# Causal attention scores for two heads in one matmul, statistics of two heads in one instruction, and a new order in the causal loops

## What is computed

```python
q, k, v = split(x @ w_qkv)                        # 16 images, 6 heads of 16 channels, 256 tokens
s = einsum("bhqd,bhkd->bhqk", q, k) * 16 ** -0.5
a = softmax(where(k_index > q_index, -1e30, s))   # causal
y = einsum("bhqk,bhkd->bhqd", a, v)
x = x + y @ w_proj
```

## Time and profile before

| | |
|---|---|
| median of three runs | 844.55 us |
| profiled execution | 844.32 us, of which the span of the core is 842.3 us |
| TensorE, VectorE, ScalarE, POOL busy in the span | 92%, 70%, 68%, 31% |
| layer 0 and the start of layer 1 | to about 82 us |
| loop of layer 1 | about 82 to 262 us |
| causal loops of layers 2 and 3 | about 310 to 455 us and 528 to 675 us |
| experts | about 695 to 842 us |

### The profile page before, as it was taken

One profiled execution on the slowest core, in us unless ns is written; L12 is line 12 of the kernel. 1 busy time (PEld: TensorE's weight loads), 2 busy tenths in 40 slices (PEclk: granted clock), 3 DMA queues, 4 the chain that ended last, 5 costly groups with the idle time before them and its releaser, 6 DMA issues.

```text
span 842.3 us, 17768 instructions
## 1 busy us (share of the span) xinstructions
PE 774.3 (92%) x5481; PEld 595.2 (71%) x5481; DVE 591.4 (70%) x1527; ACT 576.3 (68%) x1431; POOL 263.5 (31%) x514
## 2 busy tenths in 40 slices
PE   2997999999998979999999985999999978999997
PEld 1965877878886957777776683677777676777775
DVE  6157777777775447878785996688878716787775
ACT  3334878877775447878786845688888726887775
POOL 2702365665654451112121000122112110333334
PEclk9998999999999689999999987899999977999999
DMA  6000001111111123323332003132323303121320
GB/s 208 1 1 1 1 11 20 18 16 17 20 21 19 20 76 85 102 78 102 85 91 59 1 1 74 54 100 80 101 80 98 89 1 78 48 47 61 79 49 19
DMA packets 63270, 44.47 MB, mean 53 GB/s; under 512 B 34416, under 2 KB 55280, under 8 KB 63088
## 3 DMA queue, kind: packets, MB, share of 16 engines
q1 hardware_dynamic: 63216, 43.78, 20.5%
HBM read 12.24 MB, written 3.21 MB: 18 GB/s over the span
## 4 chain that ended last, share of the span: by engine, by line
PE 54%; DVE 7%; issue 3%; POOL 2%; ACT 1%; POOLq 0%
PE ps L1172 8%; PE ps L1334 8%; PE ps L1323 8%; PE ps L1045 6%; PE ps L951 5%; PE ps L955 4%; PE ps L973 2%; PE ps L974 2%; PE ps L1017 2%; PE ps L987 2%; POOL onn L416 1%; PE ps L996 1%; PE ps L1308 1%; DVE amax L1747 1%; PE ps L1093 1%
## 5 line engine op out<-in xcount | busy, mean ns | idle before, releaser
L588 ACT ACTIVATE ee<-ps,nmax 128x128 f32<-128x128 f32 (+1 forms) x584 | 207.4, 444 | 9.9 <-DVE nmax L1502 5.1
L1172 PE MATMUL ps<-w,ee 128*128 128x128 f32 x960 | 140.9, 275 | 2.5
L1172 PEld LDWEIGHTS ps<-w,ee 128*128 128x128 f32 x960 | 113.6, 143 | 19.1 <-ACT ee L588 5.0
L1505 DVE TENSOR_REDUCE nmax<-ps 128x2 f32<-128x256 f32 x200 | 101.8, 551 | 30.0 <-PE ps L955 29.1
L575 ACT ACTIVATE big<-ps 128x512 f32<-128x512 f32 (+1 forms) x192 | 97.5, 552 | 31.6 <-PE ps L1172 30.9
L1847 DVE TENSOR_TENSOR hhl<-ee,hhl 128x512 fp32r<-128x512 f32 x96 | 79.8, 837 | 32.1 <-ACT hhl L815 30.5
L944 PE MATMUL ps<-kh,big 128*128 128x256 f32 x384 | 94.7, 391 | 1.7 <-POOL big L354 1.2
L492 POOL TENSOR_TENSOR xc<-big,xc 96x512 f32<-96x512 f32 x32 | 52.6, 1643 | 108.0 <-DVE big L1841 107.9
L1502 DVE TENSOR_REDUCE nmax<-ps 128x4 f32<-128x1024 f32 x48 | 58.7, 1223 | 39.1 <-PE ps L944 38.6
L1323 PE MATMUL ps<-qk,w1hl 128*128 128x512 f32 x288 | 85.0, 406 | 0.4 <-DVE ee L1850 0.4
L1334 PE MATMUL ps<-hhl,w2hl 128*96 128x512 f32 x288 | 83.4, 400 | 0.3 <-DVE hhl L1847 0.3
(11 more groups left out here) (264 smaller groups left out, 1375.4 us busy)
## 6 DMA issues: line engine op xcount, KB each, us to landing
qk<-hl SPq DMA_DIRECT2D x288, 96.0 KB, 3.1
big<-moe_gate SPq DMA_DIRECT2D x8, 768.0 KB, 6.9
w<-w_in SPq DMA_DIRECT2D x1, 1735.0 KB, 12.9
xc<-x_in SPq DMA_DIRECT2D x4, 384.0 KB, 6.1
l_mix<-on SPq DMA_DIRECT2D x32, 48.0 KB, 2.1
tok<-l_mix SPq DMA_DIRECT2D x16, 96.0 KB, 2.0
out<-xc SPq DMA_DIRECT2D x8, 192.0 KB, 2.1
w<-w_in SPq DMA_DIRECT2D x1, 998.0 KB, 9.4
```

The source lines that it names most:

```text
L588: last = nc.scalar.activation(ee[:, ke, hh, qc, 0:w], src, ACT.Exp, bias=nmax[:, kp, hh, qc:qc + 1])
L1172: last = nc.tensor.transpose(ps[:, 4 + hh, b * P:(b + 1) * P], ee[:, u, hh, qc, tc * P:(tc + 1) * P], ident)
L1505: last = V.tensor_reduce(out=nmax[:, kp, :, qc], in_=ps[:, 2 * kp:2 * kp + 2, qc * N:qc * N + scores_cols(l, qc)], axis=AX.X, op=ALU.max, ...
```

## The change

Queries and keys of both heads of a unit are laid out in `qk` so that one matmul over all 128 rows gives both heads: `qk` gets nine slots in place of six, where slot 3 + u holds the queries of both heads, slot u the keys of the one head (zero in the other's rows) and slot u + 6 the keys of the other. The weights are ordered to match (`by_slot`), so the two projections give mixed halves of queries and keys, and the scaling of the query weights takes eight instructions. In PSUM the two heads of a block of queries now share a bank (`both`), and a mask matmul covers both heads. In VectorE's list both copies of probabilities come ahead of `keys` in `u == 0`. Both groups of values run one after the other in `u == 0`, with the waits that group 0 had. In layer 1 one `bn_stats` reads two heads' elements in turn, so that its even and odd halves are the two heads, and POOL's list loses one addition and works on half the elements.

```diff
@@ -137,7 +137,7 @@
         hl = sb("hl", [C, 2, 2, 2, N], F32R)
-        qk = sb("qk", [P, 2, NH // 2, 2, N], F32R)
+        qk = sb("qk", [P, 2, 3 * NH // 2, N], F32R)
         vh = sb("vh", [P, 2, TPI, NH, 2 * HD])
...
@@ -148,8 +148,8 @@
         w1hl = sb("w1hl", [P, 2, NE * HID], F32R)
-        est = sb("est", [P, 2, TPI, NH, 6])
-        esq = sb("esq", [P, TPI * NH, 2])
+        est = sb("est", [P, 2, TPI, NH // 2, 6])
+        esq = sb("esq", [P, TPI * NH])
         ssq = sb("ssq", [P, 2, NH])
...
@@ -251,6 +251,10 @@
             return N if l == 1 else P * (qc + 1)
+
+        def both(kp, qc, w):
+
+            return ps[:, 2 * kp + qc, 0:2 * w].rearrange("p (h t) -> p h t", h=2)
...
@@ -269,13 +273,13 @@
                 sp.wait_ge(*upto(l, "hi", n + 1))
-                for t, (hq, hk) in enumerate(((0, 0), (0, 1), (1, 0), (1, 1))):
+                for t, (h0, h1) in enumerate(((0, 0), (0, 1), (1, 0), (1, 1))):
                     if t == 1:
                         sp.wait_ge(*upto(l, "lo", n + 1))
-                    parts = hl[:, par, :, :, :].rearrange("c a h x -> c (a h) x")[:, hq:hk + 3:hk + 2 - hq, :]
+                    parts = hl[:, par, :, :, :].rearrange("c a h x -> c (a h) x")[:, h0:h1 + 3:h1 + 2 - h0, :]
                     for hh in range(2):
                         r0 = hh * 4 * HD + t * HD
-                        sp.dma_start(qk[r0:r0 + HD, par, :, :, :].bitcast(F32),
+                        sp.dma_start(qk[r0:r0 + HD, par, 3 * hh:3 * hh + 6, :].bitcast(F32),
                                      parts[hh * (C // 2):(hh + 1) * (C // 2)].bitcast(F32)).then_inc(own(l, f"stacked{par}"), 16)
...
@@ -328,7 +332,7 @@
             pool.sem_inc(sg("zeroed"), START)
-            for n, t in enumerate((qh[C:P], xn[C:P, 0:B * N], xb[C:P], kh[C:P], oc[C:P], vh[:, :, :, :, :], qk[:, :, :, :, :].bitcast(F32),
+            for n, t in enumerate((qh[C:P], xn[C:P, 0:B * N], xb[C:P], kh[C:P], oc[C:P], vh[:, :, :, :, :], qk[:, :, :, :].bitcast(F32),
                       tok_all[:, 0:TPI, :], on_all[:, 0:TPI, :])):
...
@@ -382,16 +386,15 @@
                     pool.wait_ge(sg("l1_ssq_ps"), m - 1)
-                e = est[:, m % 2].rearrange("p q h (s k) -> p (q h) s k", s=2)
+                e = est[:, m % 2].rearrange("p q u (s k) -> p (q u s) k", s=2)
                 rec = orec[:, :, (m + 1) * NH:(m + 2) * NH]
-                sums = esq[:, :, 0].rearrange("p (q h) -> p q h", q=TPI)
-                link(nc.gpsimd.tensor_tensor(esq[:, :, :], e[:, :, :, 1], e[:, :, :, 1], ALU.mult))
-                link(nc.gpsimd.tensor_scalar(esq[:, :, :], esq[:, :, :], float(N // 2), None, ALU.mult))
-                link(nc.gpsimd.tensor_tensor(esq[:, :, :], esq[:, :, :], e[:, :, :, 2], ALU.add))
-                link(nc.gpsimd.tensor_tensor(esq[:, :, 0], esq[:, :, 0], esq[:, :, 1], ALU.add))
+                sums = esq[:, :].rearrange("p (q h) -> p q h", q=TPI)
+                link(nc.gpsimd.tensor_tensor(esq[:, :], e[:, :, 1], e[:, :, 1], ALU.mult))
+                link(nc.gpsimd.tensor_scalar(esq[:, :], esq[:, :], float(N), None, ALU.mult))
+                link(nc.gpsimd.tensor_tensor(esq[:, :], esq[:, :], e[:, :, 2], ALU.add))
                 link(nc.gpsimd.tensor_tensor(sums, sums, rec, ALU.mult))
                 link(nc.gpsimd.tensor_tensor(sums, sums, rec, ALU.mult))
-                nc.gpsimd.tensor_tensor(ssq[:, m % 2, :], esq[:, 0:NH, 0], esq[:, NH:, 0], ALU.add).then_inc(sg("l1_ssq"), 1)
+                nc.gpsimd.tensor_tensor(ssq[:, m % 2, :], esq[:, 0:NH], esq[:, NH:], ALU.add).then_inc(sg("l1_ssq"), 1)
...
@@ -584,7 +587,7 @@
                         w = scores_cols(l, qc)
-                        src = ps[:, 2 * kp + hh, qc * N:qc * N + w]
+                        src = ps[:, 2 * kp + hh, qc * N:qc * N + w] if l == 1 else both(kp, qc, w)[:, hh, :]
                         last = nc.scalar.activation(ee[:, ke, hh, qc, 0:w], src, ACT.Exp, bias=nmax[:, kp, hh, qc:qc + 1])
...
@@ -946,13 +949,10 @@
                         w = scores_cols(l, qc)
-                        for hh in range(2):
-                            r0 = hh * 4 * HD
-                            mm(ps[:, 2 * kp + hh, qc * N:qc * N + w], qk[r0:r0 + 4 * HD, par, u, 0, qc * P:(qc + 1) * P],
-                               qk[r0:r0 + 4 * HD, par, u, 1, 0:w], start=(qc == 0), stop=False)
-                    for hh in range(2):
-                        diag = ps[:, 2 * kp + hh, :].rearrange("p (b t) -> p b t", t=P)[:, 0::3, :]
-                        last = mm(diag, identb[:, :], mid_dim(maskb[:, :], 1, TPI), start=False, stop=True)
+                        mm(both(kp, qc, w), qk[:, par, 3 + u, qc * P:(qc + 1) * P], qk[:, par, u::6, 0:w], start=True, stop=False)
+                    for qc in range(TPI):
+                        w = scores_cols(l, qc)
+                        last = mm(both(kp, qc, w)[:, :, w - P:w], identb[:, :], mid_dim(maskb[:, :], 1, 2), start=False, stop=True)
                 last.then_inc(own(l, "s_ps"), 1)
...
@@ -970,8 +970,9 @@
                     pe.wait_ge(sg("l1_var"), n - 4)
-                mm(ps[0:C, 7, 0:N], wa(f"l{l}_q"), x, start=True, stop=True)
-                mm(ps[0:C, 7, N:2 * N], wa(f"l{l}_k"), x, start=True, stop=True).then_inc(own(l, "q_ps"), 1)
+                first, second = ("l1_q", "l1_k") if l == 1 else (f"l{l}_qk0", f"l{l}_qk1")
+                mm(ps[0:C, 7, 0:N], wa(first), x, start=True, stop=True)
+                mm(ps[0:C, 7, N:2 * N], wa(second), x, start=True, stop=True).then_inc(own(l, "q_ps"), 1)
...
@@ -1156,6 +1157,10 @@
                             pe.wait_ge(*upto(l, f"et{hh}", START + k))
+                        if l == 3 or not isinstance(i, int) or i > 0:
+                            pe.wait_ge(*upto(l, "oc", i))
+                            pe.wait_ge(*upto(l, "v_sb", i))
+                        weigh_values(l, npar, 0)
                         weigh_values(l, npar, 1).then_inc(own(l, "av"), 1)
...
@@ -1195,11 +1200,6 @@
                             outputs_back(l, i - 1)
-                    if l > 1 and u == 2:
-
-                        pe.wait_ge(*upto(l, "oc", i + 1))
-                        pe.wait_ge(*upto(l, "v_sb", i + 1))
-                        weigh_values(l, par, 0)
...
@@ -1217,6 +1217,9 @@
                         pe.wait_ge(*upto(l, f"et{hh}", START + 3 * B))
+                    pe.wait_ge(*upto(l, "oc", B))
+                    pe.wait_ge(*upto(l, "v_sb", B))
+                    weigh_values(l, (B - 1) % 2, 0)
                     weigh_values(l, (B - 1) % 2, 1).then_inc(own(l, "av"), 1)
...
@@ -1502,7 +1505,7 @@
                     for qc in range(TPI):
-                        last = V.tensor_reduce(out=nmax[:, kp, :, qc], in_=ps[:, 2 * kp:2 * kp + 2, qc * N:qc * N + scores_cols(l, qc)],
+                        last = V.tensor_reduce(out=nmax[:, kp, :, qc], in_=both(kp, qc, scores_cols(l, qc)),
                                                axis=AX.X, op=ALU.max, negate=True)
...
@@ -1616,8 +1619,10 @@
                 if l == 1:
-                    V.tensor_scalar(wa("l2_q"), wa("l2_q"), QS, None, ALU.mult).then_inc(sg("l2_wq"), 1)
-                    V.tensor_scalar(wa("l3_q"), wa("l3_q"), QS, None, ALU.mult).then_inc(sg("l3_wq"), 1)
+                    for name in ("l2", "l3"):
+                        for a, side, lo, hi in ((0, 0, 2, 3), (0, 1, 0, 2), (1, 0, 1, 3), (1, 1, 0, 1)):
+                            v = wa(f"{name}_qk{a}").rearrange("p (s d u) -> p s d u", s=2, u=3)[:, side, :, lo:hi]
+                            V.tensor_scalar(v, v, QS, None, ALU.mult).then_inc(sg(f"{name}_wq"), 1)
                 if l == 1:
...
@@ -1649,8 +1654,8 @@
                         copy_probs(0)
+                        copy_probs(1)
                         keys(l, i + 2, par, i // 2 + 1 if isinstance(i, int) else it + 1)
-                        copy_probs(1)
                     if l > 1 and u == 1:
...
@@ -1665,9 +1670,8 @@
                             dve.wait_ge(sg("l1_ssq"), i - 1)
-                        for hh in range(2):
-                            for q in range(TPI):
-                                last = V.bn_stats(est[:, par, q, 2 * u + hh, :], ee[:, u, hh, q, :])
+                        for q in range(TPI):
+                            last = V.bn_stats(est[:, par, q, u, :], ee[:, u, :, q, :].rearrange("p h t -> p t h"))
                         last.then_inc(sg("l1_est"), 1)
...
@@ -1869,18 +1873,24 @@
     w2, w3, b3 = get("L2_attn_w_attn"), get("L3_attn_qkv_w").T, get("L3_attn_qkv_b")
-    def by_side(w):
-
-        return w.reshape(-1, NH // 2, 2, HD).transpose(0, 2, 3, 1).reshape(-1, C)
+    def by_slot(q, k):
+
+        q, k = (w.reshape(-1, NH // 2, 2, HD) for w in (q, k))
+        sides = [np.stack([k[:, :, 0], q[:, :, 0]], axis=1), np.stack([q[:, :, 1], k[:, :, 1]], axis=1)]
+        slots = np.stack([s.reshape(-1, NH // 2, 2, HD) for s in sides], axis=1)
```

(18 more changed lines are left out.)

## The result

The changed kernel takes 835.09 us (median of 4 runs, 833.65 to 839.97) against 845.11 us for the kernel before on the same chip; the ratio is 0.9898, interval 0.9861 to 0.9935. The forecast was 836.5 us. The profiled execution takes 836.18 us, with a span of 834.2 us: 8.1 us less than the profiled one of before. The medians lie 10.0 us apart; the interval of the ratio is some 6 us wide, so the two figures agree within it.

What follows compares the result with a forecast made beforehand. TensorE's order was taken as the bound, with one small wait on VectorE. From 844.32 us, −9.6 − 0.3 + 1.3 + 0.6 = −8.0 gave 836.3, as median 836.5 us; range for 8 in 10: 826 to 842.5.

Steps and rivals of the forecast that it cites:

- The ring: Causal loops: VectorE's list to the maxima, then exponentials, score unit, values and projections set the period, 8.36 us against 8.68.
- What TensorE would save without it: Causal image, if TensorE alone counted: wait, score units and shape changes save 0.90 us, 8.68 to 7.78 us.
- the paired score: Causal loops: two 128-row score matmuls replace four 64-row ones, 0.345 us in place of 0.43, 0.26 for three units.
- the first rival: Causal loops: TensorE alone decides, 27.0 us saved instead of 9.6, 819 us; chance 0.13.
- The layer's end: Last image of each causal layer: savings on scores and the later value group cancel, counted as nothing.
- Layer 0: First stage: POOL's longer zeroing of qk holds a 32-element VectorE instruction longer, +1.3 us (bounds 0 and +1.4).
- Layer 1's start: Scaling the query weights: six more VectorE instructions held, going one by one behind POOL, +0.6 us.
- The bound that I did not take: Scaling the query weights: the statistics behind the scalings are held by POOL as well, +2.0 us.
- The statistics: Layer 1: paired statistics of 0.65 to 1.1 us, zero in the loop, −0.3 us at its end.
- The stacking: Causal loops: SyncE's chain of stacking DMAs moves by less than 0.1 us, wanted one image later; nothing.
- The second rival: Causal loops: paired matmuls go at half rate, a unit takes 1.01 us, loops stay as they are, 846 us; chance 0.09.
- The third: First attention's loop: strided paired statistics at 1.5 us each make VectorE set the pace, 868 us; chance 0.08.

Runs made afterwards that it cites:

- ring_dummy: Changed kernel plus one unused 384-element VectorE addition per causal image, between the normalisation and the maxima of u == 1: 856.09 us.
- copy_on_act: Changed kernel with the second copy of probabilities of u == 0 moved from VectorE to ScalarE, ScalarE's deviation steps put ahead of the high parts: 826.34 us.
- copy_on_act_old_values: The kernel of copy_on_act with the first group of values back at the end of u == 2, ahead of the score unit: 829.84 us.
- scores_alone: Changed kernel with both reorderings undone (copies and values in the old order), paired scores and statistics kept: 838.85 us.
- outside_dummy: Changed kernel plus the same unused VectorE addition as ring_dummy, but behind the statistics of u == 2, where VectorE idles: 835.82 us.

## Why the prediction was right, point by point

- *The ring.* Right as a path and in its sum. From the image's first transposes (400.94): end of the maxima predicted +3.67, measured 404.61 − 400.94 = +3.67; end of the exponentials +5.14, measured 406.09, +5.15; score unit +5.29, +5.20; values +5.96, +5.98; projections +7.42, +7.42; period 8.36, and 8.36 or 8.41. `ring_dummy` and `copy_on_act` show that VectorE's list sets the period, so the cause is shown and not only a sum that fits. Two terms were off and cancel, which is luck: the release of the score unit took 406.14 − 406.09 = 0.05 and not 0.15 us, and the unit 406.92 − 406.14 = 0.78 and not 0.665. And the waits are not all where the prediction put them: of the 8.36 − 7.94 = 0.42 us that come back (0.58 predicted), 0.53 − 0.35 = 0.18 stand ahead of the score unit; the other 0.24 stand earlier, 0.10 of them between value projections and outputs, and were not named. They cost nothing as long as the score unit has to wait for the exponentials in any case.
- *What TensorE would save without it.* Mis-sized: 0.90 us, a list of 7.78 us. The list takes some 7.94 us (`copy_on_act` without its wait), so it saves 0.74. The old wait gives 0.23 (I had 0.28) and the groups together 0.23 (two changes of shape, 0.18). The term that failed is the paired score: 0.26 for three units and 0.18 for two changes into half rows, where 8.45 − 8.17 = 0.28 us came. The unit's first matmul comes 0.20 and not 0.115 us ahead of its second, so a unit reaches its masks in 0.44 us as before; the whole saving lies in the way into it (from the outputs to the scores 0.28 us in place of 0.42), which I had counted beside the unit. It cost the forecast little, because the ring decided, and because the unit's error in the ring met the opposite one of the release; the first rival would have been 30 × 0.74 = 22 us, 824 and not 819 us.
- *The layer's end.* Counted at nothing; the last image became 0.27 us longer in each layer (7.06 to 7.33), because the value group now stands behind the last copy.
- *Layer 0.* +1.3 us predicted; 1.83 became 3.11 us.
- *Layer 1's start.* +0.6 predicted, the values' copy came 2.51 us later, of which 1.2 is layer 0's: +1.3. The bound that I did not take, the statistics held as well, is what happened: before, four of them had started by 68.4 us under the held scaling and ended with it; now they start at 71.21, behind the scalings, and take their 1.33 us there. The +0.6 for six more scalings did not come: all eight end at 71.33, 0.14 us behind POOL's memset, so the sum is +1.3 and not that bound's +2.0.
- *The statistics.* 693 ns, at the low end of 0.65 to 1.1 us, against 2 × 412 ns for two heads. The rule of the Trainium skill that was weighed (SBUF — State Buffer, "Door 1: The DMA port swizzle", a penalty for every change of 16-byte line) is not borne out by this read: with a change of line at every element it took 693 / 512 = 1.35 ns an element, and 412 / 256 = 1.61 ns in a row. A read of 512 elements in a row was not run. POOL's shorter list gave 1.92 − 1.54 = 0.38 us (0.3).
- *The stacking.* The issues start 0.90 us after the first transposes as before, and the scores do not wait for them.

The terms in sum: periods −9.0 (predicted −9.6), layers' ends +0.5 (0), ahead of layer 2 +0.7 (+1.6), between the layers −0.35, the rest +0.1: −8.05, of 8.1 measured. Ahead of layer 2 the edits themselves cost 1.9 us: +2.5 at the second score block (77.90 to 80.42), −0.26 in the first loop, −0.38 at its end. The other −1.2 us come from the granted clock: the eight transposes at the first loop's start took 1.44 us before and 0.88 after (81.47 to 82.91, 83.95 to 84.83), the six ahead of the first outputs 1.27 and 0.66 (316.04 to 317.31, 317.34 to 318.00). The granted clock there, before and after (it is the column behind POOL's): the lower of its two levels and the full one, with TensorE busy throughout in both:

```profile
316.00:318.00 2.00, 2.00 (x11) 1.83 (x9) 1.08 (x3) 1.72 (x5) 0.00 (x0) 0.50 0.00 0
316.00:318.00 2.00, 2.00 (x20) 1.48 (x14) 0.13 (x1) 1.05 (x2) 0.00 (x0) 1.00 0.00 0
```

No term of the prediction had this. Without it and without the stretch between the layers, whose cause is open, the profiled execution would have gained 6.5 us: that the sum met −8.0 is in part luck. The 1.7 us that a measurement of this kernel was said to tell are too few: the ratio's interval is 3 us to either side. The second rival (pairing buys nothing) fell with `copy_on_act_old_values`; as long as the copies are in the old order it is half right, as `scores_alone` shows (8.55 us, of 0.28 saved only 0.13 reach the period). The third fell with the 693 ns.

## What to carry to other kernels

Where one engine is busy 99% of the time, look for a ring through the others before pricing its instructions: sum the list of each engine from one event to the same event of the next turn. Of three edits to one loop, the swap of two VectorE instructions brought most of the gain, and taking one more copy out of VectorE's part of the ring brought another 7 to 9 us with TensorE's list as it was. Put a large memset where its engine and its neighbour are both idle.

## What the runs showed of the hardware

The same stretch can run at another clock in another run. In the two windows behind layer 1's loop, which no edit touches, the granted clock was 0.77 and 0.78 in the changed kernel and 0.91 and 1.00 in `copy_on_act`, so at the lower of the two levels (1.2 and 2.4 GHz) for part of both windows in the one, and for part of the first window only in the other. In both, TensorE had waits in the first window, 14.3 and 14.4 of 18 us busy:

```profile
262.00:280.00 18.00, 14.31 (x100) 11.75 (x98) 7.38 (x27) 8.13 (x22) 6.58 (x25) 0.77 0.15 24
280.00:300.00 20.00, 20.00 (x140) 19.51 (x140) 8.99 (x52) 9.77 (x26) 10.28 (x18) 0.78 0.19 42
```

```profile
262.00:280.00 18.00, 14.44 (x124) 12.08 (x123) 7.76 (x34) 8.84 (x25) 8.02 (x29) 0.91 0.17 29
280.00:300.00 20.00, 16.36 (x138) 15.34 (x137) 11.89 (x68) 11.85 (x32) 11.39 (x18) 1.00 0.27 67
```

The first score unit of layer 2 came 5.1 us earlier in `copy_on_act` (308.63 to 303.53), though the kernels differ only behind that point, and TensorE's wait behind layer 1's loop ended only 0.6 us earlier (270.95 to 270.36). So edits of 1 to 3 us are judged by rows here and not by medians.

One VectorE addition of 384 elements took 0.54 us at one place of the loop and 0.55 to 0.79 us at another; the difference goes with what POOL did beside it:

```profile
406.62 0.54 DVE L1671 TENSOR_TENSOR scr<-ones 128x384 f32<-128x384 f32 x1
```

```profile
326.67 0.55 DVE L1650 TENSOR_TENSOR scr<-ones 128x384 f32<-128x384 f32 x1
```

In `outside_dummy` (first row) POOL was idle beside 31 of the 32 additions, and all took 0.54 or 0.55 us. In `ring_dummy` POOL's `tensor_tensor` on `onn` was running when 28 of the 32 began, and these took 0.66 to 0.79 us, longer the more of it was left; the four others took 0.55 us (second row), among them two beside which a POOL copy began. So a part of the 0.62 us that `ring_dummy` added to the period goes with this meeting, and only 0.54 is the addition's own length.
